# Wide-head attention written step by step, with queries and keys of two tiles at once in three split passes

## The chip, the cores and the metric

The kernel runs on one core of one Trainium2 chip. The metric is the device time of one execution in microseconds. TensorE is PE in the rows (PEld is its weight load), VectorE is DVE, ScalarE is ACT, GpSimd is POOL and SyncE is SP.

## What is computed

The reference is a stack of four layers, each a cross-attention or a mixture stage followed by a feed-forward stage, over 32 sequences of 64 rows with 128 features (2,048 rows). The stage that is changed is the attention of the second layer. Its shape, cut from the reference:

```python
DIM = 128
NUM_HEADS = 16
DIM_HEAD = 64
INNER = NUM_HEADS * DIM_HEAD
SCALE = DIM_HEAD ** (-0.5)
def _layernorm(x, gamma, beta, eps=1e-05):
    mu = jnp.mean(x, axis=-1, keepdims=True)
    var = jnp.mean(jnp.square(x - mu), axis=-1, keepdims=True)
    return (x - mu) * jax.lax.rsqrt(var + eps) * gamma + beta
```

A row is normalised twice (once outside, once with `gamma` and `beta`), projected to 1,024 query columns; the context of the same sequence is projected to 1,024 key and 1,024 value columns. Each of the 16 heads takes a softmax over the 64 keys of the sequence, and the 1,024 results are projected back to 128, scaled by a gate and added to the row.

## The kernel before

The 2,048 rows are 16 tiles of 128 rows (two sequences each). The stages run one after the other: A0 (attention with small heads), F0 (a feed-forward, during which a router for a later stage is worked out "beside" it), A1 (the wide-head attention that is changed, `wide_head_attention`), E1 (16 experts), then E2, E3, A3 and Q3. Every engine has one instruction queue, in program order, and the engines meet only through semaphores. What runs when is thus set by the order in which each engine's part of a stage is written.

A1 is a software pipeline. Every engine executes the same sequence of steps `n`, and in a step it serves several tiles at different stages of their way. In step n, PE does `scores(n-2)`, `turn_x(n-1)` (a transpose of the normalised tile), `turn_probs(n-3)`, `queries(n-1)`, `turn_out(n-4)`, `keys(n)`, `weigh_values(n-3)`, `project(n-4)` and `values(n-2)`. Queries and keys are 8 fp32 matmuls of 128x128 by 128 columns each, per tile. DVE does in step n: `x1` (the outer normalisation applied to tile n), the inner statistics, maximum and subtraction on the scores of tile n-2, the inner normalisation applied, the outer statistics of tile n+1, sum and reciprocal of the softmax, the scaling of the weighted values, the addition to X, and two copies of the values out of PSUM. POOL does `inner.rstd(n)`, `outer.rstd(n+1)` (a power on a 128x1 column, each waiting for DVE's statistics), and a copy of the context tile (`ctx1`) for `values`. ACT copies everything else out of PSUM and takes the exponentials. Steps 0 to 6 and 15 to 20 are written out; steps 7 to 14 are a loop of two steps per iteration (`pipeline`, L48), whose addresses and wait values come from registers. PSUM banks J0 and J1 are shared in turn by the turned x, queries, keys and values of a step; the waits in `keys`, `queries`, `turn_x` and `values` on `q_ready`, `k_ready` and `v_ready` hand them over.

In F0, products with 512 columns are already done in three passes of the type float32r (high times high, high times low, low times high): the low part of the input is made by POOL in `low_part` (L249), by a subtraction of two SBUF operands. POOL's part of F0 ends with the four `owners` (L1922) of the router, which take what DVE makes in `places` (L1910, L1914) and give it to PE's `table_products` (L1930). DVE's chain of small router operations (`choose`, L1818 to L1846), then the addition of the bias to X (L1687), then `slots` (L1876 to L1890) stand ahead of those in its queue; PE's `rank_products` (L1865) wait for the last link of `choose`.

## Time and profile before

| | us |
|---|---|
| median of 3 runs | 962.73 |
| lowest and highest | 961.08, 964.19 |
| span of the profiled execution, first to last instruction | 1010.8 |
| of it F0 (from the end of A0 at 100.0) | about 48 |
| of it A1, from its first product (148.36) to E1's first router product (344.08) | 195.7 |

Only the span is given for the profiled execution; it is 48 us longer than the median of the runs without a profile. In the span, PE is busy for 77%, DVE for 60%, ACT for 48% and POOL for 37%, and the chain that ended last is PE for 67%. These are averages over stages of very different kinds; A1 by itself is read from windows and the timeline. Times in the rows are microseconds from the span's start.

### The profile page before, as it was taken

What the parts mean: (1) busy time and instruction counts of PE and PEld (TensorE: products, weight loads), DVE (VectorE), ACT (ScalarE), POOL (GpSimd) and SP (SyncE); (2) the same over time, 40 slices, a digit from 0 to 9 for tenths busy, and PEclk for the clock granted to TensorE, in tenths of its full rate; (3) what the DMA queues carried; (4) which work ended last, traced back from release to release, by engine and by line L of the source; (5) the groups of instructions that cost most, each with busy time, mean ns of one, the idle gap of its engine ahead of it and who ended that gap; (6) DMA issues with size and microseconds to landing.
All of it is one profiled execution on the core that took longest, in us unless ns stands there. A gap on an engine that the chain in (4) does not pass through costs nothing.

```text
span 1010.8 us, 24129 instructions
## 1 busy us (share of the span) xinstructions
PE 783.2 (77%) x8041; PEld 646.4 (64%) x8041; DVE 608.2 (60%) x1568; ACT 486.4 (48%) x984; POOL 372.9 (37%) x492
## 2 busy tenths in 40 slices
PE   6998899999999789996477775667677559969005
PEld 3766787888888679985476664667676526644005
DVE  3886747777777667767353224632222368867895
ACT  3886434555444344432154435334444357745753
POOL 5663421111111331111566653155556535550810
PEclk9999699999999979999699989579989769978557
DMA  6300000000000000033332213101111300000001
GB/s 187 96 0 1 1 1 3 2 3 0 0 0 3 1 11 19 21 102 103 95 100 88 64 41 105 42 19 43 40 37 45 85 23 3 0 1 1 0 0 42
DMA packets 49218, 36.06 MB, mean 36 GB/s; under 512 B 7665, under 2 KB 44978, under 8 KB 49138
## 3 DMA queue, kind: packets, MB, share of 16 engines
q1 hardware_dynamic: 43420, 24.45, 8.5%
q0 software_dynamic: 4992, 10.23, 3.6%
q8 instruction: 48, 0.79, 0.3%
q10 hardware_dynamic: 726, 0.33, 0.1%
q14 instruction: 32, 0.26, 0.1%
HBM read 26.73 MB, written 8.26 MB: 35 GB/s over the span
## 4 chain that ended last, share of the span: by engine, by line
PE 67%; DVE 9%; another core or an unknown queue 6%; issue 5%; ACT 5%; DMA 3%; DVEq 2%; POOL 2%; ACTq 1%; SPq 1%; POOLq 0%
PE psum L2118 9%; PE psum L1464 7%; PE psum L2143 4%; PE psum L1034 3%; PE psum L976 3%; PE psum L954 3%; PE psum L939 3%; PE psum L2442 2%; PE psum L1431 2%; PE psum L1432 2%; PE psum L1433 2%; PE psum L323 2%; PE psum L1016 2%; PE psum L663 2%
## 5 line engine op out<-in xcount | busy, mean ns | idle before, releaser
L2118 PE MATMUL psum<-E_XT,E_weights 128*128 128x128 f32 x780 | 114.3, 298 | 52.4 <-ACT E_XT L2198 27.7
L2118 PEld LDWEIGHTS psum<-E_XT,E_weights 128*128 128x128 f32 x780 | 103.0, 209 | 61.2 <-ACT E_XT L2198 30.8
L2266 POOL DMA_INDIRECT y_scratch<-E_y,route_place_of x78 | 78.8, 1010 | 83.2 <-DVE E_y L2321 37.8
L2258 POOL DMA_INDIRECT E_rows<-rows_scratch,route_token_of x78 | 76.4, 979 | 32.1 <-issue 25.5
L1723 DVE SCALAR_TENSOR_TENSOR X<-psum,E_gates,X 128x128 f32<-128x128 f32 x256 | 71.7, 344 | 26.5 <-PE psum L1464 26.4
L1464 PEld LDWEIGHTS psum<-E_w,E_h 128*128 128x128 f32 x512 | 69.4, 198 | 11.5 <-issue 3.5
L2221 ACT ACTIVATE E_h<-psum,cols 128x128 f32<-128x128 f32 x156 | 44.5, 368 | 66.4 <-issue 31.3
L1548 ACT ACTIVATE E_h<-psum,cols 128x512 f32<-128x512 f32 x64 | 43.8, 687 | 67.8 <-PE psum L1433 67.7
L1464 PE MATMUL psum<-E_w,E_h 128*128 128x128 f32 x512 | 70.4, 282 | 4.8 <-DVE X L1723 3.8
L2311 DVE TENSOR_TENSOR E_h<-E_sg,psum 128x384 f32<-128x384 f32 x39 | 21.6, 554 | 77.5 <-remote 26.8
L203 POOL TENSOR_TENSOR rstd<-vareps,nhalf 128x4 f32<-128x4 f32 x24 | 24.6, 1029 | 75.0 <-DVE vareps L197 74.9
L235 PE MATMUL psum<-ident,xn 128*128 128x128 f32 x80 | 20.0, 400 | 35.9 <-ACT xn L226 24.5
L2143 PE MATMUL psum<-L1w,E_h 128*128 x312 | 44.4, 288 | 0.5 <-DVE E_y L2323 0.5
L150 POOL TENSOR_TENSOR A_A_inner_rstd<-A_A_inner_vareps,nhalf 128x1 f32<-128x1 f32 x16 | 8.7, 543 | 95.5 <-DVE A_A_inner_vareps L144 95.5
L788 POOL TENSOR_TENSOR A_kexp<-E_first,hmask 128x512 f32<-128x512 f32 x32 | 32.7, 1042 | 30.0 <-PE psum L663 29.9
L2431 PE MATMUL psum<-ident,Q_amax_rows 128*1 128x128 f32 x5 | 1.7, 332 | 52.1 <-DVE Q_amax_rows L2539 51.4
L235 PEld LDWEIGHTS psum<-ident,xn 128*128 128x128 f32 x80 | 14.0, 210 | 43.5 <-issue 21.5
L2323 DVE TENSOR_TENSOR E_y<-psum,E2b2all 128x128 f32<-128x128 f32 x39 | 11.3, 290 | 49.6 <-PE psum L2143 27.9
L2143 PEld LDWEIGHTS psum<-L1w,E_h 128*128 128x128 f32 x312 | 40.4, 202 | 1.0 <-issue 0.7
L2114 PE MATMUL psum<-ident,E_rows 128*128 128x128 f32 x78 | 22.8, 293 | 22.3 <-DMA E_rows<-rows_scratch,route_token_of 22.3
L2204 ACT ACTIVATE E_weights<-E_first 128x768 f32 x39 | 32.9, 843 | 14.2 <-issue 13.9
L1075 ACT ACTIVATE A_xnT<-psum,cols 128x128 f32<-128x128 f32 x16 | 7.3, 457 | 65.3 <-PE psum L964 65.3
(346 smaller groups left out, 2160.2 us busy)
## 6 DMA issues: line engine op xcount, KB each, us to landing
routed_back<-y_scratch SPq DMA_DIRECT2D x16, 256.0 KB, 4.9
E_first<-in_L_xattn_W SPq DMA_DIRECT2D x1, 2048.0 KB, 8.6
L1w<-in_L_xattn_W SPq DMA_DIRECT2D x8, 256.0 KB, 4.7
rows_scratch<-xn SPq DMA_DIRECT2D x8, 256.0 KB, 2.3
E_w<-in_L_ffn_routed_w SPq DMA_DIRECT2D x28, 64.0 KB, 1.9
E_raw<-in_L_ffn_w_down SPq DMA_DIRECT2D x8, 176.0 KB
E_rows<-rows_scratch,route_token_of POOLq DMA_INDIRECT x78
y_scratch<-E_y,route_place_of POOLq DMA_INDIRECT x78
```

Source lines behind the costliest of these rows:

```text
L235: tr = pe.transpose(self.bank[:, i * P:(i + 1) * P], self.m.xn[:, g * GT + i, :], self.m.ident[:, :])
L788: ke = pool.tensor_tensor(kexp[:, p, b], kk.broadcast_to([P, HP, S]), m.hmask[:, :].rearrange("p (h o) -> p h o", o=1).broadcast_to([P, HP ...
L939: mm = pe.matmul((J1, J0)[j][:, c * P:(c + 1) * P], w["k"][:, cc * P:(cc + 1) * P], columns(m.ctxT, t, P), start=True, stop=True)
L1464: mm = pe.matmul(y_bank(e, g)[:, i * P:(i + 1) * P], h[:, g % 2, c, i * P:(i + 1) * P], w2[:, p, c, :], start=(c == 0 and i == 0), stop=(c ...
L1548: act.activation(h[:, g % 2, c, :], ring[(C * g + c) % 4], spec["func"], bias=spec["b1"][:, bass.ds(e * C + c, 1)]).then_inc(h_ready.sem, 1)
L1723: st = dve.scalar_tensor_tensor(out=m.X[:, t, :], in0=y_bank(e, g)[:, i * P:(i + 1) * P], scalar=gates[:, t, bass.ds(e, 1)], in1=m.X[:, t, :],
L2118: mm = pe.matmul(out[:, c * P:(c + 1) * P], WE[:, p, (k0 + c) * P:(k0 + c + 1) * P], XT[:, p, :], start=True, stop=True)
L2143: mm = pe.matmul(Y[p][:, 0:P], h[:, p, c, :], W2[:, bass.ds(e, 1), c, :].rearrange("p o d -> p (o d)"), start=c == 0, stop=c == C - 1)
L2204: act.activation(WE[:, i % 2, :], W1[:, bass.ds(e, 1), :].rearrange("p o f -> p (o f)"), ACT.Copy).then_inc(w_ready.sem, 1)
L2221: ac = act.activation(h[:, p, c, :], m.banks[2 + i % 3][:, c * P:(c + 1) * P], spec["func"], bias=spec["b1"][:, bass.ds(e * C + c, 1)])
L2258: pool.indirect_dma_start(out=xg[:, i % 4, :], out_offset=None, in_=rows[:, :], in_offset=bass.IndirectOffsetOnAxis(ap=disp.token_of[:, i: ...
L2266: pool.indirect_dma_start(out=yrows[:, :], in_=y[:, i % 3, :], in_offset=None, out_offset=bass.IndirectOffsetOnAxis(ap=disp.place_of[:, i: ...
```

## The change

A1 is written out for all its steps, 23 instead of 21, without a loop. The weights of queries and keys are split into a high part (rounded to float32r, made by ACT in two copies of 128x1024 ahead of F0) and a low part (made by POOL in two subtractions of 128x1024, written between F0's `low_part` and its `owners`). The context is split by four ACT copies of 128x512 (`CH`) after F0's ACT work, and four POOL subtractions of 128x512 (`CL`) ahead of A1's first `outer.rstd`. The normalised tile is copied out of PSUM by two ACT activations instead of one (`xH`, `xnT`), and POOL subtracts them (`x_low`, 128x128), as the third thing of its step, where the copy of the context tile stood. Queries and keys are made for a pair of tiles at once: in each step half of a pair's keys and half of a pair's queries, 4 blocks of 3 passes by 256 columns each. So `scores` runs four steps behind `x1` instead of two. `queries` of a pair need the low parts of both its tiles: in an even step n, that of tile n-1, which the same step turns. The keys of the first pair stand ahead of A1's start. Large buffers are laid over others that are free at the time (F0's weights move to a place of their own for it), and `values` reads the context itself.

```diff
-def wide_head_attention(sh, m, tag, start, w):
...
+def wide_head_attention(sh, m, tag, start, w, split_weights):
...
-        qT = sb("qT", [P, 2, HP, P])
-        ctx1 = sb("ctx1", [P, 2, P])
-        kT = sb("kT", [P, 2, HP, 2, S])
+        q_odd = sb("qT", [P, HP, PW])
+        k_odd = sb("kT", [P, HP, PW])
...
+    qT = [m.xn[:, :, :].rearrange("p t d -> p (t d)").rearrange("p (c q) -> p c q", q=PW), q_odd]
+    kT = [m.XNT[:, :].rearrange("p (c k) -> p c k", k=PW), k_odd]
+    xH, xL = (m.split_rows[:, i, :].rearrange("p (r q) -> p r q", q=PW) for i in range(2))
+    CH, CL = m.split
+    WH, WL = m.wide_high, m.wide_low
...
     def tensor(pe):
-        m.begin(pe, start)
         pe.wait_ge(*m.dispatch.owner_ready(1))
-
-        def keys(t, p):
+        pe.wait_ge(*split_weights)
+
+        def three(out, wk, cc, xs, start=True):
+            ws = slice(cc * P, (cc + 1) * P)
+            pe.matmul(out, WH[:, wk, ws], xs[0], start=True, stop=False)
+            pe.matmul(out, WH[:, wk, ws], xs[1], start=False, stop=False)
+            return pe.matmul(out, WL[:, wk, ws], xs[0], start=False, stop=True)
+
+        def keys(i, n):
+            pair, half = i // 2, i % 2
+            cols = slice(pair * PW, (pair + 1) * PW)
+            pe.wait_ge(*ctx_low(pair // 2 + 1))
             for j in range(2):
-                if past(t, 1):
-                    pe.wait_ge(*q_ready(2 * t - 1 + j))
-                for c in range(4):
-                    cc = 4 * j + c
-                    mm = pe.matmul((J1, J0)[j][:, c * P:(c + 1) * P], w["k"][:, cc * P:(cc + 1) * P],
-                                   columns(m.ctxT, t, P), start=True, stop=True)
+                if i == 1:
+                    pe.wait_ge(*k_ready(j + 1))
+                elif i >= 2 and j == 1:
+                    pe.wait_ge(*xnT_ready(n))
+                elif i >= 2 and n >= 5:
+                    pe.wait_ge(*v_ready(2 * (n - 5) + 1))
+                elif i >= 2:
+                    pe.wait_ge(*q_ready(2 * (n - 3) + 1))
+                for c in range(2):
+                    mm = three((J1, J0)[j][:, c * PW:(c + 1) * PW], 1, 4 * half + 2 * j + c, (CH[:, cols], CL[:, cols]))
                 mm.then_inc(k_ps.sem, 1)
 
...
+        def turn_x(t, n, p):
+            pe.wait_ge(*xn_ready(t + 1))
+            if n >= 5:
+                pe.wait_ge(*v_ready(2 * (n - 5) + 2))
...
+            pe.transpose(J0[:, 0:P], xn[:, p, :], m.ident[:, :]).then_inc(xnT_ps.sem, 1)
+
+        def queries(i, n):
+            pair, half = i // 2, i % 2
+            r = pair % 2
+            pe.wait_ge(*x_low(2 * pair + 2))
...
+                for c in range(2):
+                    mm = three((J1, J0)[j][:, c * PW:(c + 1) * PW], 0, 4 * half + 2 * j + c, (xH[:, r, :], xL[:, r, :]))
+                mm.then_inc(q_ps.sem, 1)
...
                 for u in range(2):
-                    mm = pe.matmul((J1, J0)[b][u * S:(u + 1) * S, :], ctx1[:, p, b * S:(b + 1) * S], wv[:, :, u, :],
-                                   start=True, stop=True)
+                    mm = pe.matmul((J1, J0)[b][u * S:(u + 1) * S, :], m.ctxT[:, t * P + b * S:t * P + (b + 1) * S],
+                                   wv[:, :, u, :], start=True, stop=True)
                 mm.then_inc(v_ps.sem, 1)
...
+        for i in range(2):
+            keys(i, 0)
+        m.begin(pe, start)
+
...
-            if begun(n) and n == NT + 2:
+            if is_tile(n - 4):
+                scores(n - 4)
+            if is_tile(n - 1):
+                turn_x(n - 1, n, q)
+            if is_tile(n - 5):
+                turn_probs(n - 5, q)
...
+            if 3 <= n <= NT:
+                keys(n - 1, n)
+            if is_tile(n - 6):
+                turn_out(n - 6, p)
+            if is_tile(n - 2):
+                queries(n - 2, n)
+            if is_tile(n - 5):
+                weigh_values(n - 5, q)
+            if after(tag) and n == NT + 5:
+                after(tag).turn(pe, 1)
+            if is_tile(n - 6):
+                project(n - 6, p)
+            if is_tile(n - 4):
+                values(n - 4, n)
+
+        steps(step)
...
     def scalar(act):
+        for s, n in first_products_done:
+            act.wait_ge(s, n)
+        for g in range(NG):
+            cols = slice(g * GW, (g + 1) * GW)
+            act.activation(CH[:, cols], m.ctxT[:, cols], ACT.Copy).then_inc(ctx_high.sem, 1)
+
+        def keys_kept(i):
+            pair, half = i // 2, i % 2
+            if pair >= 2:
+                act.wait_ge(*scores_ready(2 * pair - 2))
+            for j in range(2):
+                c = 4 * half + 2 * j
+                act.wait_ge(*k_ps(2 * i + j + 1))
+                act.activation(kT[pair % 2][:, c:c + 2, :].rearrange("p c k -> p (c k)"), (J1, J0)[j],
+                               ACT.Copy).then_inc(k_ready.sem, 1)
+
+        for i in range(2):
+            keys_kept(i)
         m.begin(act, start)
...
+            if is_tile(n - 1):
                 t = n - 1
                 act.wait_ge(*xnT_ps(t + 1))
-                if past(t, 2):
-                    act.wait_ge(*q_ps(2 * t - 2))
+                if t >= 4:
+                    act.wait_ge(*q_ps(4 * (t // 2) - 4))
+                act.activation(xH[:, t // 2 % 2, t % 2 * P:(t % 2 + 1) * P], J0[:, 0:P], ACT.Identity, bias=w["beta"],
+                               scale=w["gamma"])
+                if t >= 2:
+                    act.wait_ge(*x_low(t - 1))
                 act.activation(xnT[:, q, :], J0[:, 0:P], ACT.Identity, bias=w["beta"],
                                scale=w["gamma"]).then_inc(xnT_ready.sem, 1)
...
-        pipeline(act, step, LO, HI, END)
+            if after(tag) and NT + 4 <= n < NT + 6:
+                after(tag).evacuate(act, n - NT - 4)
+
+        steps(step)
...
     def gpsimd(pool):
+        for g in range(NG):
+            cols = slice(g * GW, (g + 1) * GW)
+            pool.wait_ge(*ctx_high(g + 1))
+            pool.tensor_tensor(CL[:, cols], m.ctxT[:, cols], CH[:, cols], ALU.subtract).then_inc(ctx_low.sem, 1)
         m.begin(pool, start)
...
         def step(n, p):
-            if live(n):
+            if is_tile(n):
                 inner.rstd(pool, n, p, xn_ready)
-            if live(n + 1):
+            if is_tile(n + 1):
                 outer.rstd(pool, n + 1, 1 - p, x1_ready)
-            if live(n - 1):
-                context(n - 1, 1 - p)
+            if is_tile(n - 1):
+                t = n - 1
+                at = slice(t % 2 * P, (t % 2 + 1) * P)
+                pool.wait_ge(*xnT_ready(t + 1))
+                pool.tensor_tensor(xL[:, t // 2 % 2, at], xnT[:, 1 - p, :], xH[:, t // 2 % 2, at],
+                                   ALU.subtract).then_inc(x_low.sem, 1)
 
         outer.rstd(pool, 0, 0, x1_ready)
-        pipeline(pool, step, LO, HI, END)
-        if begun(NT):
+        steps(step)
...
-                t = n - 2
+            if is_tile(n - 4):
+                t = n - 4
                 dve.wait_ge(*scores_ready(t + 1))
...
                 split(pool, e + 1, 1)
         if beside:
+            spec["pool_between"](pool)
...
+        with ExitStack() as early:
+            m.wide_low = early.enter_context(nc.sbuf_tensor("L1w_low", [P, 2, 1024], F32R))
...
+        with ExitStack() as early:
+            m.split_rows = early.enter_context(nc.sbuf_tensor("A1_xnT_split", [P, 2, 4 * P], F32R))
+        with ExitStack() as early:
+            f0_weights = early.enter_context(nc.sbuf_tensor("F0_weights", [P, 2, 4 * P], F32))
+            m.wide_high = early.enter_context(nc.sbuf_tensor("L1w_high", [P, 2, 1024], F32R))
...
+        wide_high_ready, wide_low_ready = sem("wide_high_ready"), sem("wide_low_ready")
+
+        def low_parts(pool):
+            for i, k in enumerate((1, 0)):
+                pool.wait_ge(wide_high_ready, i + 1)
+                pool.tensor_tensor(m.wide_low[:, k, :], wide[:, k, :], m.wide_high[:, k, :], ALU.subtract
+                                   ).then_inc(wide_low_ready, 1)
+
...
+                            "F0": (f0_weights[:, 0:1, :], f0_weights[:, 1:2, :].rearrange("p o (c d) -> p o c d", d=D))}
...
+            for k in (1, 0):
+                act.activation(m.wide_high[:, k, :], wide[:, k, :], ACT.Copy).then_inc(wide_high_ready, 1)
```

POOL's queue at the end of F0 and the start of A1, before (`F_XL` is F0's low part, `route_A` the owners, the `rstd` rows the normalisation of A1's tiles, `A_ctx` the copied context tile):

```order
L249 TENSOR_TENSOR F_XL<-XNT,F_XH 128x512 x3
L1922 TENSOR_TENSOR route_A<-route_is_block,token_number 128x320 x4
L150 TENSOR_TENSOR A_A_outer_rstd<-A_A_outer_vareps,nhalf 128x1
L150 TENSOR_TENSOR A_A_inner_rstd<-A_A_inner_vareps,nhalf 128x1
...
L1124 COPY A_ctx<-ctxT 128x128
```

The same queue now (`L1w_low` is the low part of the weights, `E_XL` as written here the low part of the context, `A_xnT_split` the low part of a normalised tile):

```order
L249 TENSOR_TENSOR F_XL<-XNT,F_XH 128x512 x3
L2913 TENSOR_TENSOR L1w_low<-L1w,L1w_high 128x1024 x2
L1971 TENSOR_TENSOR route_A<-route_is_block,token_number 128x320 x4
L1167 TENSOR_TENSOR E_XL<-ctxT,E_XH 128x512 x4
L150 TENSOR_TENSOR A_A_outer_rstd<-A_A_outer_vareps,nhalf 128x1
L150 TENSOR_TENSOR A_A_inner_rstd<-A_A_inner_vareps,nhalf 128x1
...
L1179 TENSOR_TENSOR A_xnT_split<-A_xnT,A_xnT_split 128x128
```

Two subtractions came in ahead of the owners, four ahead of A1's first normalisation, and one per tile behind the two `rstd` of its step.

PE's queue in one full step of A1, before (`A_qT`, `A_kT` are queries and keys in SBUF, `A_on` the scaled result, `A_oT` the same turned):

```order
L990 MATMUL psum<-A_kT,A_qT 64x64 x32
L964 MATMUL psum<-ident,A_xn 128x128
L1001 MATMUL psum<-ident,A_prob 128x128 x8
L976 MATMUL psum<-A_xnT,L1w 128x128 x8
L1027 MATMUL psum<-ident,A_on 128x128 x8
L939 MATMUL psum<-ctxT,L1w 128x128 x8
L1016 MATMUL psum<-A_v,A_probT 64x64 x32
L1034 MATMUL psum<-L1w,A_oT 128x128 x8
L954 MATMUL psum<-L1w,A_ctx 64x512 x4
```

And in one full step now; of four blocks of keys (`E_XH`, `E_XL`) and four of queries (`A_xnT_split`) the first three passes stand (`XNT` and `xn` hold every second pair's keys and queries):

```order
L1013 MATMUL psum<-XNT,xn 64x64 x32
L971 MATMUL psum<-ident,A_xn 128x128
L1024 MATMUL psum<-ident,A_prob 128x128 x8
L940 MATMUL psum<-E_XH,L1w_high 128x256
L941 MATMUL psum<-E_XL,L1w_high 128x256
L942 MATMUL psum<-E_XH,L1w_low 128x256
...
L1050 MATMUL psum<-ident,A_on 128x128 x8
L940 MATMUL psum<-A_xnT_split,L1w_high 128x256
L941 MATMUL psum<-A_xnT_split,L1w_high 128x256
L942 MATMUL psum<-A_xnT_split,L1w_low 128x256
...
L1039 MATMUL psum<-A_v,A_probT 64x64 x32
L1057 MATMUL psum<-L1w,A_oT 128x128 x8
L998 MATMUL psum<-L1w,ctxT 64x512 x4
```

Keys and queries changed places around the turning of the result; the other rows stand as they stood.

## Rows read from the trace of the kernel before

**Rows 1.** Windows: stretch, length, busy time per engine, PEclk (granted clock), DMA share, GB/s.

```profile
173.40:314.50 141.10, 140.23 (x2418) 118.51 (x2416) 107.82 (x217) 69.40 (x120) 15.29 (x35) 1.00 0.01 1
```

**Rows 2.** Timeline of PE, a written-out step of A1: start, length, instruction, count.

```profile
185.97 1.16 PE L990 MATMUL psum<-A_kT,A_qT 64*64 64x64 f32 x64
...
188.10 1.95 PE L976 MATMUL psum<-A_xnT,L1w 128*128 128x128 f32 x16
...
189.89 1.04 PE L1027 MATMUL psum<-ident,A_on 128*128 128x128 f32 x8
...
190.76 1.95 PE L939 MATMUL psum<-ctxT,L1w 128*128 128x128 f32 x16
...
192.65 1.16 PE L1016 MATMUL psum<-A_v,A_probT 64*64 64x64 f32 x64
...
197.59 1.16 PE L990 MATMUL psum<-A_kT,A_qT 64*64 64x64 f32 x64
```

**Rows 3.** Timeline of E1: three passes by 512 columns, one after the other.

```profile
376.90 0.48 PE L1431 MATMUL psum<-E_XH,E_WH 128*128 128x512 f32 x1
377.21 0.40 PE L1432 MATMUL psum<-E_XL,E_WH 128*128 128x512 f32 x1
377.45 0.39 PE L1433 MATMUL psum<-E_XH,E_WL 128*128 128x512 f32 x1
```

**Rows 4.** Timeline of DVE and POOL in the step of rows 2.

```profile
187.80 1.23 DVE L1157 TENSOR_REDUCE A_mx<-psum 128x16 f32<-128x1024 f32 x1
...
191.34 0.54 POOL L150 TENSOR_TENSOR A_A_outer_rstd<-A_A_outer_vareps,nhalf 128x1 f32<-128x1 f32 x1 [2.84 <-DVE A_A_outer_vareps L144]
```

**Rows 5.** Timeline of E1's start: POOL's subtraction of 128x128.

```profile
345.96 0.46 POOL L1581 TENSOR_TENSOR E_WL<-E_w,E_WH 128x128 fp32r<-128x128 f32 x1
```

**Rows 6.** Timeline of F0: POOL's last subtraction, and DVE's router chain.

```profile
117.00 1.27 POOL L249 TENSOR_TENSOR F_XL<-XNT,F_XH 128x512 fp32r<-128x512 f32 x1 [1.08 <-ACT XNT L243]
117.08 1.34 DVE L1837 SCALAR_TENSOR_TENSOR route_at<-route_first,route_logits 128x128 f32<-128x128 f32 x1
...
119.10 0.29 DVE L1821 TENSOR_TENSOR route_work<-route_work,rev 128x128 f32<-128x128 f32 x1
...
121.26 2.28 DVE L1687 TENSOR_TENSOR X<-X,F0b 128x2048 f32<-128x2048 f32 x1
```

**Rows 7.** Timeline of F0, later: the slots, the second owner, the first table.

```profile
124.18 0.17 DVE L1876 TENSOR_SCALAR route_ntile<-psum 128x8 f32<-128x8 f32 x1 [0.64 <-PE psum L1867]
...
132.71 0.72 POOL L1922 TENSOR_TENSOR route_A<-route_is_block,token_number 128x320 fp32r<-128x320 f32 x1 [0.61 <-DVE route_is_block L1914]
...
133.84 1.94 PE L1930 MATMUL psum<-route_A,route_B 128*128 128x40 f32 x16
```

**Rows 8.** Timeline where A1 begins: ACT's last of F0, then POOL, ACT, DVE.

```profile
145.47 0.22 ACT L1851 ACTIVATE route_gate<-route_gate 128x16 f32<-128x16 f32 x1
...
149.33 0.55 POOL L150 TENSOR_TENSOR A_A_outer_rstd<-A_A_outer_vareps,nhalf 128x1 f32<-128x1 f32 x1 [9.73 <-DVE A_A_outer_vareps L144]
...
149.64 0.60 ACT L1107 ACTIVATE A_kT<-psum 128x512 f32<-128x512 f32 x1 [3.96 <-PE psum L939]
...
149.91 0.34 DVE L154 TENSOR_SCALAR A_x<-X,A_A_outer_meanvar,A_A_outer_rstd 128x128 f32<-128x128 f32 x1 [0.76 <-POOL A_A_outer_rstd L150]
...
153.50 0.34 DVE L154 TENSOR_SCALAR A_x<-X,A_A_outer_meanvar,A_A_outer_rstd 128x128 f32<-128x128 f32 x1 [0.65 <-POOL A_A_outer_rstd L150]
```

**Rows 9.** Windows with the granted clock, columns as in rows 1.

```profile
349.70:356.00 6.30, 5.06 (x17) 4.24 (x18) 1.88 (x4) 1.53 (x3) 3.87 (x5) 0.50 0.00 1
581.20:584.60 3.40, 3.40 (x18) 3.40 (x17) 0.78 (x2) 1.14 (x4) 2.34 (x3) 0.50 0.15 43
593.10:596.50 3.40, 3.38 (x28) 3.32 (x29) 0.92 (x3) 1.14 (x4) 2.49 (x4) 1.00 0.23 60
```

**Rows 10.** Timeline of PE: the idle time (in brackets) ahead of such windows.

```profile
349.76 1.09 PE L235 MATMUL psum<-ident,xn 128*128 128x128 f32 x4 [2.93 <-issue]
...
580.22 1.21 PE L2118 MATMUL psum<-E_XT,E_weights 128*128 128x128 f32 x8 [2.08 <-DVE E_XT L2296]
```

225 lines of the change are left out of this document (96 added, 129 removed).

## The prediction

> **What bounds the kernel now.** I read the windows first. A1's twelve full steps, from the scores of tile 2 to those of tile 14, take 141.1 us, and PE is busy for 140.2 of them at a granted clock of 1.00 (2.4 GHz), DVE for 107.8, ACT for 69.4, POOL for 15.3 [rows 1]. So in A1 the end is set by PE's own queue, and a matmul saved there is time saved as long as PE waits for nobody. The timeline of a written-out step shows the queue [rows 2]: scores, turned x and turned probabilities 2.13 us (185.97 to 188.10), queries 1.79, turned result 0.87, keys 1.89, then weighted values, projection and values 4.94; together 11.62. The loop's steps come to about 0.14 more (141.1 / 12 = 11.76). DVE and POOL are off the path, but their place in the step matters below: POOL's `outer.rstd` starts 5.37 us after the scores and had waited 2.84 us for DVE's outer statistics, which stand behind the maximum and the subtraction on this step's scores [rows 4].
>
> **PE's saving.** A pair costs, for queries and keys, 8 blocks of 3 passes by 256 columns each. No row has 256 columns. The nearest are passes by 512 at intervals of 0.31 (the first after fp32) and 0.24 us [rows 3]. The bounds are half of that, 0.12, if time goes with columns, and 0.24, if it does not. I take 0.12: 512 columns at 2.4 GHz are 0.213 us, so nearly all of the interval is columns. 12 passes are 1.45 us where 16 fp32 halves took 1.79 to 1.89. A step that waits for nothing is 2.13 + 1.45 + 0.87 + 1.45 + 4.94 = 10.84.
>
> The rows of 512 columns run at 0.24. The Trainium skill (TensorE: Matmul & The Clock Gate, Back-to-back issue gap) gives columns / 2.4 + 2.5 ns, 0.216 for 512; the row is longer. By it, 256 columns would be 0.109 and 12 passes 1.31, and the forecast some 2.3 us lower; the row decides.
>
> **The wait that is added.** In an even step PE's queries need the low part of the tile turned in the same step. POOL makes it, behind `outer.rstd` of the next tile but one in its queue. That ends 5.37 + 0.54 = 5.91 us after the scores [rows 4], the subtraction of 128x128 is 0.46 [rows 5], and two handovers bring it to 6.5. PE reaches its queries at 2.13 + 1.45 + 0.87 = 4.45. It then stands 2.05 us, with weighted values, projection, values and the next scores behind it: 6.5 + 1.45 + 4.94 = 12.9. This length no longer holds the price of the keys. DVE can't come earlier: its maximum waits for this step's scores, and ahead of it stand the copies of the values, which end with PE's last step. In odd steps the pair's low parts are there. A pair is 12.9 + 10.84 = 23.7, against 23.2 to 23.5 before: what the passes save, the wait gives back.
>
> From step 6 (the first full one) to step 17 (no keys, as step 16 before) there are eleven steps: 6, 8, 10, 12 and 14 wait; in 16 no `outer.rstd` is left. 5 x 12.9 + 6 x 10.84 = 129.5, where twelve took 141.0: -11.5. The queries of the last step save 0.35. ACT copies the turned x twice now, ahead of the probabilities that PE waits for. One copy is at most 0.60 [rows 8], and only the six steps without the other wait could feel it: 0 to 3.6 in all; I take 0, since ACT is busy for half of rows 1.
>
> **What it costs ahead of that: F0.** POOL's subtractions of 512 columns take 1.27 us, and a DVE operation on two SBUF operands that fell on one ran 1.34 instead of 0.29, until POOL was through [rows 6]. The two subtractions of 1,024 columns (2.54 each) now follow at once. The first holds DVE's next such operation from 118.42 to 120.96, the second holds L1821, at 119.10 so far, until 123.79: +4.69. DVE's bias addition then ends at 128.23, and the slots begin at 128.27 instead of 124.18: +4.1 [rows 6, 7]. The first table on PE stands 0.4 behind the second owner, which stands on the slots [rows 7]; it moves by 4.1 and F0's end with it, since PE is packed from there on. Bounds: 0, if all of it is hidden, and 5.1, the whole length of the two.
>
> That a subtraction of 2.54 us holds DVE to its end no row shows; rows 6 show it for 1.27. The Trainium skill (SBUF — State Buffer, SBUF: two separate sides) says that the loser waits for the whole instruction. If it were held for 1.27 alone, F0 would move by 1.6, and the forecast be 2.5 us lower; I go by the whole.
>
> **The context's low parts.** ACT's last work of F0 ends at 145.69 + 4.1 = 149.8; a copy of 512 columns is 0.60 [rows 8]; POOL then subtracts four times 1.27, from 150.45 to 155.55, ahead of A1's first `outer.rstd`. That was at 149.33 and comes at 155.6: 2.2 on top of the 4.1. Bounds 0 and 5.1.
>
> **Filling the pipeline.** DVE's first `x1` is then at 156.2. Without scores in between a tile takes 3.59 us [rows 8], so tile 2 is at 163.4, `outer.rstd` of tile 3 ends at 166.95, the low part of tile 1 follows, and the first queries start at 167.5. PE has had 2.9 us of keys and two transposes in 15 us. After 2.93 us of idling a stretch at 0.50 (1.2 GHz) followed [rows 9, 10], so I put these queries at half clock, 2.7 us instead of 1.45. With the copies (0.60 each) and the next keys and queries handing J0 and J1 to each other, scores of tile 0 are at 175.7 (174.2 at full clock). From them to the next `outer.rstd`'s end is 1.2 + 4.08 (187.80 to 191.88, rows 4), so step 4's queries start at 181.6, after PE idled for 3.1 us. Queries, copy and values bring step 5 to 185.0; it has no projection and is 8.0 long. Step 6: 193.0. For the clock after the 3.1 us I add 1.7, what 3.4 us at 0.50 lose [rows 9]: 194.7. From `x1` that is 38.5; before it was 149.91 to 173.43, 23.5: +15.0. Bounds: +11.8 without the clock, +18 if it stays low until step 6.
>
> **Sum.** +4.1 + 2.2 + 15.0 - 11.5 - 0.35 = +9.4 us at E1's start, and nothing behind it changes. The span of the profile is 1010.8 and the median 962.73; A1 ran at full clock in the profile, so I add the sum as it is: 962.7 + 9.4 = 972.1. About 0.3% (2.9 us) is what a measurement here can tell from no change.
>
> **Rivals.**
> 1. The passes pay and the low part is no wait. The mechanism is A1's wait on `x_low`: it decides at 4.45 us after the scores. If DVE and POOL reach `outer.rstd` 2 us sooner than rows 4 show, all eleven steps are 10.84 (119.2, 10.3 less) and step 4's idling goes (4.8 less): 957.0, faster. For it speaks PE's busy share in rows 1; against it the order on POOL and DVE. 0.10.
> 2. F0 and the context hide: the table has slack, or POOL's subtractions find DVE on single operands. 6.3 less: 965.8. 0.15, half of it within 0.3%.
> 3. The clock falls in the stalls of the even steps too. After an idle time of 2.08 us the stretch 581.2 to 584.6 was at 0.50, after another of that kind (593.1) the clock stayed at 1.00 [rows 9, 10]. Five falls at 1.7: 980.6. 0.15.
> 4. The change doesn't do what it says, a pass of 256 costs the 0.24 of 512: 12 are 2.82, an odd step 13.6, an even one 14.3, together 153.1: 995.7. Against it the arithmetic of columns above. 0.05.
>
> **How the numbers follow.** The forecast, 972.1, holds 0.55; it spreads by the bounds of the fill and of F0 from 965 to 977. The range, 963 to 982, takes in rivals 2 and 3; it leaves out rivals 1 and 4 and little more. Faster by over 0.3%: rival 1, 0.10. Within: half of rival 2 and the forecast's lower edge, 0.10. Slower: 0.80.
>
> **What will show it.** In the changed profile: PE's idle time in even steps, some 2 us ahead of the queries' first pass, released by POOL's `A_xnT_split`, and none in odd ones; starts of scores 12.9 and 10.8 us apart in turn; passes 0.12 apart; DVE's L1821 and the one before it stretched to some 2 us; the first table near 137.9; A1's first `outer.rstd` near 155.6; PEclk 0.50 around 167. It is wrong if the low part lands before PE asks for it, or if the F0 chain takes the two subtractions in its stride.

## The result, and the profile after

| | before | after |
|---|---|---|
| median of 4 runs, us | 963.15 | 978.74 |
| lowest and highest | 961.08, 964.19 | 978.47, 981.53 |
| ratio, with its 95% interval | | 1.017 (1.014 to 1.020) |

The changed kernel is 15.6 us slower. Its profiled execution took 978.51 us, with a span of 976.8. The span of before was 48 us above its median, and behind the end of E1 its trace is 51 us longer than that of the changed kernel (518.8 against 467.7); so the two traces are compared stage by stage and no further than the end of E1.

The steady part first, from scores of tile 2 to scores of tile 14, as in [rows 1]. Window of the changed kernel, columns as there:

```profile
194.01:334.57 140.56, 130.41 (x2306) 107.80 (x2304) 102.87 (x197) 70.15 (x128) 14.95 (x30) 1.00 0.01 2
```

The stretch is 140.6 us, 141.0 before [rows 1]. PE's work fell from 140.2 to 130.4, and its idle time rose from 0.9 to 10.2: the passes pay, and the wait takes it back. An even step in the timeline (PE and POOL of step 6):

```profile
194.01 1.16 PE L1013 MATMUL psum<-A_kT,A_qT 64*64 64x64 f32 x64
...
199.39 0.54 POOL L150 TENSOR_TENSOR A_A_outer_rstd<-A_A_outer_vareps,nhalf 128x1 f32<-128x1 f32 x1 [2.85 <-DVE A_A_outer_vareps L144]
199.89 0.45 POOL L1179 TENSOR_TENSOR A_xnT_split<-A_xnT,A_xnT_split 128x128 fp32r<-128x128 f32 x1
...
200.40 0.39 PE L940 MATMUL psum<-A_xnT_split,L1w_high 128*128 128x256 f32 x1 [1.81 <-POOL A_xnT_split L1179]
200.62 0.28 PE L941 MATMUL psum<-A_xnT_split,L1w_high 128*128 128x256 f32 x1
200.74 0.28 PE L942 MATMUL psum<-A_xnT_split,L1w_low 128*128 128x256 f32 x1
...
206.96 1.16 PE L1013 MATMUL psum<-A_kT,A_qT 64*64 64x64 f32 x64
```

POOL's `outer.rstd` waits 2.85 us for DVE's variance, as before ([rows 4], 2.84). The low part stands behind it, and PE stands for that: 1.81 us, released by `A_xnT_split`. The step is 12.95 long, the odd one behind it 10.86. The passes are 0.12 apart.

F0, DVE's router chain and POOL beside it, then PE (compare [rows 6, 7]):

```profile
118.06 4.85 POOL L2913 TENSOR_TENSOR L1w_low<-L1w,L1w_high 128x1024 fp32r<-128x1024 f32 x2
118.61 2.04 DVE L1868 TENSOR_TENSOR route_work<-route_at,route_best 128x128 f32<-128x128 f32 x1
120.68 2.37 DVE L1870 TENSOR_TENSOR route_work<-route_work,rev 128x128 f32<-128x128 f32 x1
...
124.91 2.28 DVE L1736 TENSOR_TENSOR X<-X,F0b 128x2048 f32<-128x2048 f32 x1
...
124.96 0.49 PE L1914 MATMUL psum<-route_both,earlier 128*128 128x128 f32 x2 [1.50 <-DVE route_ahead L1893]
...
133.52 1.64 POOL L1971 TENSOR_TENSOR route_A<-route_is_block,token_number 128x320 fp32r<-128x320 f32 x1 [10.61 <-DVE route_is_block L1963]
```

Two DVE operations of the kind that takes 0.29 us [rows 6] took 2.04 and 2.37 beside POOL's two subtractions. The bias addition, at 121.26 before, starts at 124.91; and PE now idles for 1.50 us ahead of the router's products.

The first and the third owner and DVE's last addition of F0, before, and then the last two of these after:

```profile
130.46 1.64 POOL L1922 TENSOR_TENSOR route_A<-route_is_block,token_number 128x320 fp32r<-128x320 f32 x1 [12.19 <-DVE route_is_block L1914]
...
136.63 1.64 POOL L1922 TENSOR_TENSOR route_A<-route_is_block,token_number 128x320 fp32r<-128x320 f32 x1 [3.20 <-DVE route_is_block L1914]
...
147.62 0.69 DVE L1719 TENSOR_TENSOR X<-X,psum 128x512 f32<-128x512 f32 x1 [4.67 <-PE psum L1464]
```

```profile
138.35 1.64 POOL L1971 TENSOR_TENSOR route_A<-route_is_block,token_number 128x320 fp32r<-128x320 f32 x1 [1.87 <-DVE route_is_block L1963]
...
149.45 0.69 DVE L1768 TENSOR_TENSOR X<-X,psum 128x512 f32<-128x512 f32 x1 [4.67 <-PE psum L1512]
```

The first owner is 3.1 us later, the third 1.7 and the last addition 1.8 (0.1 more each, counted from the mark that follows below): POOL waited 3.20 us ahead of the third owner before and waits 1.87 now, so part of the delay ends there.

The beginning of A1 on POOL and DVE, and then PE in the fill (compare [rows 8]):

```profile
148.12 5.00 POOL L1167 TENSOR_TENSOR E_XL<-ctxT,E_XH 128x512 fp32r<-128x512 f32 x4 [6.79 <-ACT E_XH L1097]
...
150.84 0.15 DVE L144 TENSOR_SCALAR A_A_outer_vareps<-A_A_outer_meanvar 128x1 f32<-128x1 f32 x1
...
153.07 0.55 POOL L150 TENSOR_TENSOR A_A_outer_rstd<-A_A_outer_vareps,nhalf 128x1 f32<-128x1 f32 x1
```

```profile
156.13 0.30 PE L971 MATMUL psum<-ident,A_xn 128*128 128x128 f32 x1 [3.22 <-DVE A_xn L154]
159.49 0.47 PE L971 MATMUL psum<-ident,A_xn 128*128 128x128 f32 x1 [3.06 <-DVE A_xn L154]
165.00 0.58 PE L940 MATMUL psum<-A_xnT_split,L1w_high 128*128 128x256 f32 x1 [5.04 <-POOL A_xnT_split L1179]
165.38 0.41 PE L941 MATMUL psum<-A_xnT_split,L1w_high 128*128 128x256 f32 x1
165.60 0.42 PE L942 MATMUL psum<-A_xnT_split,L1w_low 128*128 128x256 f32 x1
...
173.33 1.16 PE L1013 MATMUL psum<-XNT,xn 64*64 64x64 f32 x64 [0.78 <-ACT xn L1152]
...
179.28 0.58 PE L940 MATMUL psum<-A_xnT_split,L1w_high 128*128 128x256 f32 x1 [2.66 <-POOL A_xnT_split L1179]
...
182.14 3.52 PE L998 MATMUL psum<-L1w,ctxT 128*64 128x512 f32 x8
```

The variance was there at 150.99, `outer.rstd` came at 153.07 behind the four low parts of the context. The first queries run at half clock (a granted clock of 0.50; passes 0.21 apart), after 5.04 us of idling, and so do step 4's queries and values (3.52 us for eight products that otherwise take 1.94), after 2.66.

E1 is 2.5 us shorter in these two traces. Windows of the changed kernel from E1's first expert product on:

```profile
373.33:377.33 4.00, 3.06 (x8) 1.96 (x9) 3.56 (x6) 2.18 (x3) 4.00 (x5) 0.60 0.01 2
377.33:381.33 4.00, 4.00 (x31) 3.74 (x31) 3.00 (x9) 1.63 (x3) 4.00 (x7) 1.00 0.00 0
```

and the same two stretches of the kernel before:

```profile
353.75:357.75 4.00, 3.06 (x8) 1.95 (x8) 3.56 (x6) 2.18 (x3) 4.00 (x5) 0.50 0.01 2
357.75:361.75 4.00, 4.00 (x16) 3.71 (x17) 3.01 (x9) 1.02 (x2) 4.00 (x7) 0.50 0.00 0
```

The same work, after the same 2.93 us of idling; the clock is back in the second window of the changed kernel and not yet in that of before. From E1's first router product to PE's first work on what E1 leaves behind it is 147.94 us before and 145.42 after. The change is not shown to be the cause: the second of these windows in two of the kernels that follow, e1 and then e6, with 148.42 and 145.32 us for the same code:

```profile
358.66:362.66 4.00, 4.00 (x16) 3.71 (x17) 3.01 (x9) 1.02 (x2) 4.00 (x7) 0.50 0.00 0
```

```profile
356.20:360.20 4.00, 4.00 (x31) 3.74 (x31) 3.01 (x9) 1.63 (x3) 4.00 (x7) 1.00 0.00 0
```

**All stages in one table.** F0 begins up to 3.8 us sooner or later from execution to execution, so I count from a mark, POOL's third `rstd` of F0 (its line L203, at 104.51 before and 104.40 after). The columns follow each other: to A1's first `outer.rstd`; from there to scores of tile 0, and to scores of tile 2 (the fill); from scores of tile 2 to 14; from there to E1's first router product; E1. The last but one is the sum without the column of tile 0, the last the median of the runs. The kernels e1 to e9 are the experiments below. Each batch of runs has its own runs of the kernel before, with medians of 963.15 (for the changed kernel), 962.38 (e1 to e4), 961.42 (e5 to e7) and 962.84 (e8 and e9); every ratio is to those of its batch. One of the four runs of e4 took 1187.3 us at a granted clock of 0.631 and is left out of its median.

| kernel | to rstd | tile 0 | tile 2 | 12 steps | tail | E1 | sum | median |
|---|---|---|---|---|---|---|---|---|
| before | 44.82 | 7.55 | 24.10 | 141.03 | 29.62 | 147.94 | 387.51 | 963.15 |
| after | 48.67 | 20.26 | 40.94 | 140.56 | 29.09 | 145.42 | 404.68 | 978.74 |
| e1, low part first | 48.64 | 17.49 | 32.67 | 129.97 | 29.08 | 148.42 | 388.78 | 961.53 |
| e2, weights late | 46.72 | 21.71 | 40.86 | 142.10 | 29.08 | 145.93 | 404.69 | 977.97 |
| e3, context spread | 46.80 | 22.05 | 42.60 | 140.60 | 29.08 | 145.25 | 404.33 | 979.75 |
| e4, clock kept | 51.67 | 19.05 | 36.93 | 142.11 | 29.08 | 145.47 | 405.26 | 979.97 |
| e5, context early | 49.73 | 20.27 | 40.72 | 140.61 | 29.07 | 145.29 | 405.42 | 981.08 |
| e6, three moves | 43.74 | 18.40 | 33.57 | 129.98 | 29.07 | 145.32 | 381.68 | 957.22 |
| e7, and clock | 43.75 | 15.92 | 31.08 | 129.97 | 29.09 | 147.48 | 381.37 | 956.14 |
| e8, e6 without e1 | 44.72 | 20.26 | 41.00 | 140.58 | 29.08 | 145.73 | 401.11 | 976.43 |
| e9, queries sooner | 44.31 | 15.13 | 31.05 | 129.97 | 29.09 | 145.30 | 379.72 | 956.47 |

At E1's start the changed kernel has lost 3.85 + 16.84 - 0.47 - 0.53 = 19.7 us; E1 is 2.5 shorter, which leaves 17.2 in these two executions, where the medians have 15.6. E1 is the same code in all of the rows. It takes 147.5 to 148.4 us in the three executions in which the clock came back late (before, e1, e7) and 145.3 to 145.9 in the other eight. So 2.5 us of a difference between two single traces can come of E1 alone; where the rest of the way from 19.7 to 15.6 lies, these two traces don't show.

### The profile page after: what moved, and what is told of

It is laid out like the page before. It is cut to its first block, busy times and chain, and to the rows that moved or that the text cites. A ratio compares the mean times of both kernels' runs of the same rounds, so it can differ in the third digit from the quotient of the medians.

```text
span 976.8 us, 23579 instructions
## 1 busy us (share of the span) xinstructions
PE 766.5 (78%) x7913; PEld 625.0 (64%) x7913; DVE 613.5 (63%) x1568; ACT 495.3 (51%) x1006; POOL 384.3 (39%) x498
## 4 chain that ended last, share of the span: by engine, by line
PE 48%; issue 19%; POOL 13%; DVE 9%; ACT 5%; DMA 4%; SPq 1%; ACTq 1%; DVEq 0%; POOLq 0%
PE psum L1512 7%; POOL y_scratch L2315 4%; PE psum L2167 4%; POOL E_rows L2307 4%; PE psum L2192 3%; PE psum L2491 2%; PE psum L323 2%; PE psum L1481 2%; PE psum L1479 2%; PE psum L1480 2%; PE psum L1057 2%; PE psum L373 2%; PE psum L1862 1%; PE psum L663 1%; PE psum L349 1%
## 5 line engine op out<-in xcount | busy, mean ns | idle before, releaser
L2167 PE MATMUL psum<-E_XT,E_weights 128*128 128x128 f32 x780 | 103.9, 282 | 1.5 <-DVE E_XT L2345 0.8
L2167 PEld LDWEIGHTS psum<-E_XT,E_weights 128*128 128x128 f32 x780 | 96.7, 198 | 2.9 <-DVE E_XT L2345 1.5
L203 POOL TENSOR_TENSOR rstd<-vareps,nhalf 128x4 f32<-128x4 f32 x24 | 24.6, 1029 | 92.9 <-DVE vareps L197 92.8
L2163 PE MATMUL psum<-ident,E_rows 128*128 128x128 f32 x78 | 22.8, 292 | 24.2 <-DMA E_rows<-rows_scratch,route_token_of 24.1
L1627 POOL CAST E_WH<-E_w 128x128 fp32r<-128x128 f32 x16 | 4.6, 290 | 89.4 <-DMA E_w<-in_L_ffn_routed_w 69.7
L2192 PE MATMUL psum<-E_last,E_h 128*128 x234 | 34.5, 284 | 5.9 <-DVE E_h L2360 2.6
```

Source lines behind the costliest of these rows:

```text
L203: pool.tensor_tensor(m.rstd[:, ts], m.vareps[:, ts], m.nhalf[:, :].broadcast_to([P, GT]), ALU.pow).then_inc(self.rstd_ready.sem, 1)
L2167: mm = pe.matmul(out[:, c * P:(c + 1) * P], WE[:, p, (k0 + c) * P:(k0 + c + 1) * P], XT[:, p, :], start=True, stop=True)
L2192: mm = pe.matmul(Y[p][:, 0:P], h[:, p, c, :], W2[:, bass.ds(e, 1), c, :].rearrange("p o d -> p (o d)"), start=c == 0, stop=c == C - 1)
```

## The experiments

**The low part first (e1).** Theory: PE's wait in even steps is POOL's order alone. Rival: the two banks that go through ACT would hold PE there anyway.

```diff
         def step(n, p):
-            if is_tile(n):
-                inner.rstd(pool, n, p, xn_ready)
-            if is_tile(n + 1):
-                outer.rstd(pool, n + 1, 1 - p, x1_ready)
             if is_tile(n - 1):
                 t = n - 1
...
                 pool.tensor_tensor(xL[:, t // 2 % 2, at], xnT[:, 1 - p, :], xH[:, t // 2 % 2, at],
                                    ALU.subtract).then_inc(x_low.sem, 1)
+            if is_tile(n):
+                inner.rstd(pool, n, p, xn_ready)
+            if is_tile(n + 1):
+                outer.rstd(pool, n + 1, 1 - p, x1_ready)
```

> POOL makes the low part of the turned tile at the head of its step, ahead of inner.rstd and outer.rstd; nothing else is changed against the changed kernel (978.7 us). Theory A, that the even steps' 1.8 us and step 4's 2.7 us on PE are POOL's queue order alone: the low part then lands about 3.3 us after the scores where PE asks at 4.4, scores stand 10.9 us apart in every step of the steady part (twelve steps 130.5 instead of 140.6, that is -10 to -12), step 4 loses its 2.7 us of idling and perhaps its half clock (-2.7 to -5.6), and the first queries start 3.7 us sooner because tile 1's low part no longer stands behind the third outer.rstd (-2 to -3.7). Together 957 to 963 us. Theory B, that the handover of the two banks through ACT (keys copied, then queries into the same bank) would hold PE there anyway: the idle time stays at about 1.8 us, now released by ACT, and the time stays within 4 us of 978.7.

Measured: 961.53 us, 17.2 less than the changed kernel, and 1.0005 of the kernel before (0.9975 to 1.0036). The steady part as a window, and step 6 in the timeline:

```profile
185.94:315.91 129.97, 129.08 (x2305) 107.63 (x2303) 102.92 (x197) 70.16 (x128) 14.95 (x30) 1.00 0.01 3
```

```profile
185.94 1.16 PE L1013 MATMUL psum<-A_kT,A_qT 64*64 64x64 f32 x64
...
188.28 0.46 POOL L1175 TENSOR_TENSOR A_xnT_split<-A_xnT,A_xnT_split 128x128 fp32r<-128x128 f32 x1 [4.85 <-ACT A_xnT L1124]
...
190.28 0.36 PE L940 MATMUL psum<-A_xnT_split,L1w_high 128*128 128x256 f32 x1
...
191.32 0.54 POOL L150 TENSOR_TENSOR A_A_outer_rstd<-A_A_outer_vareps,nhalf 128x1 f32<-128x1 f32 x1 [2.09 <-DVE A_A_outer_vareps L144]
...
196.81 1.16 PE L1013 MATMUL psum<-A_kT,A_qT 64*64 64x64 f32 x64
```

The low part is done 2.8 us after the scores, PE takes it at 4.34 without idling, and every step is 10.87 long: 10.6 us less in twelve. The fill is 8.3 us shorter, since tile 1's low part no longer waits for the third `outer.rstd` and step 4 no longer idles. The rival falls, and the time is within theory A's 957 to 963. The low part's place in POOL's queue cost 18.9 us up to E1's start, of the 19.7 lost there.

**The weights' low parts late (e2).** Theory: they hold the router's chain in F0, and that moves A1. Rival: the table has slack.

```diff
         if beside:
-            spec["pool_between"](pool)
             for j in range(NCH):
                 beside.owners(pool, j)
+            spec["pool_between"](pool)
```

> POOL's two subtractions of 1,024 columns (low parts of the weights) stand behind the four owner operations of F0 instead of ahead of them. Theory A, that they stretched two DVE operations of the table (2.04 and 2.37 us where 0.29 is usual) and that this moved the table by 3.05 us, F0's last addition by 1.8 and A1's first outer.rstd by the rest: those two operations are back at 0.29, the owners are back within 0.3 of 130.5 and 132.7, the context's low parts start at 145.1, A1's first outer.rstd is at 150.0 instead of 153.07, and the time is 975.7 (974.5 to 976.9). Theory B, that the table had slack and the context's low parts set A1's start for another reason: the owners move back, the first outer.rstd does not, and the time stays at 978.7.

Measured: 977.97 (ratio to before 1.0145, 1.0107 to 1.0182), above theory A's 974.5 to 976.9 and, by the interval, not to be told from the changed kernel. The trace tells more: the two DVE operations are back at 0.29 us, the first owner is 25.95 us after the mark, as before (25.95; after 29.12), PE doesn't idle ahead of the router's products, and `outer.rstd` is 1.95 us sooner, not 3.05. The context's low parts still stand ahead of it, and they wait for ACT's copies behind the read-out of the table, which moved by 1.96. In this execution the clock fell once in an even step; windows of step 6, which was 14.43 long and idled 1.82 us ahead of its queries:

```profile
189.98:196.00 6.02, 4.58 (x95) 4.27 (x93) 5.58 (x13) 3.84 (x8) 1.17 (x3) 1.00 0.01 3
196.00:198.00 2.00, 1.62 (x9) 1.62 (x10) 0.67 (x2) 0.24 (x1) 0.32 (x1) 0.71 0.00 0
198.00:200.00 2.00, 2.00 (x46) 1.77 (x48) 0.00 (x0) 1.38 (x3) 0.00 (x0) 0.50 0.00 0
200.00:202.00 2.00, 2.00 (x46) 1.93 (x41) 1.21 (x1) 0.52 (x1) 0.00 (x0) 0.94 0.03 8
```

That is 1.5 us, once. So theory A holds for the table, and its size for A1's start was less.

**The context's low parts spread (e3).** Theory: four in a row keep the first `outer.rstd` waiting. Rival: something else sets the fill.

```diff
...
+        context_low(0)
         m.begin(pool, start)
...
                 inner.rstd(pool, n, p, xn_ready)
+            if 1 <= n < NG:
+                context_low(n)
```

> Only the first of the context's four low parts stands ahead of A1's first outer.rstd on POOL; the other three follow one by one behind inner.rstd of tiles 1 to 3. Theory A, that the four in a row (5.0 us) kept outer.rstd waiting behind a variance that DVE had ready at 150.99: outer.rstd starts at 151.0 instead of 153.07, each later subtraction delays the next outer.rstd by 0.1 to 0.2, and the time falls by 1.5 to 2.1, to about 977. Theory B, that the fill of the pipeline is set by something other than that chain of tiles: outer.rstd moves and scores of tile 0 stay at 173.3, the time at 978.7. A third way: POOL's subtractions hold DVE's operations in the fill, which then costs 1 us or more per subtraction: 979 to 981.

Measured: 979.75 (ratio 1.0174, 1.0140 to 1.0209). `outer.rstd` starts 1.87 us sooner, and scores of tile 0 are where they were, counted from the mark. The time alone (977.20 to 980.97 in four runs) fits theory B's 978.7 as well as the third way's 979 to 981; the trace shows the third way's mechanism. DVE and POOL in the fill:

```profile
152.62 0.34 DVE L154 TENSOR_SCALAR A_xn<-A_x,A_A_inner_meanvar,A_A_inner_rstd 128x128 f32<-128x128 f32 x1 [0.67 <-POOL A_A_inner_rstd L150]
...
156.11 1.26 POOL L1167 TENSOR_TENSOR E_XL<-ctxT,E_XH 128x512 fp32r<-128x512 f32 x1
156.18 1.27 DVE L154 TENSOR_SCALAR A_xn<-A_x,A_A_inner_meanvar,A_A_inner_rstd 128x128 f32<-128x128 f32 x1 [0.66 <-POOL A_A_inner_rstd L150]
```

DVE's `xn`, the operation that POOL had just released, takes 1.27 us instead of 0.34 beside each of the three subtractions, and the chain from one tile to the next grows by 0.9 three times.

**The clock kept up in the fill (e4).** Theory: the half clock of the first queries comes of the idling. Rival: it doesn't.

```diff
             if is_tile(n - 1):
                 turn_x(n - 1, n, q)
+            if n == 2:
+                for _ in range(38):
+                    pe.matmul(pO[:, 0, 0:PW], WH[:, 1, 0:P], CH[:, 0:PW], start=True, stop=True)
```

and 24 of the same ahead of `turn_x` in steps 1 and 2.

> PE runs passes of 256 columns on the context in the idle time of the fill (24 ahead of each of the first two turned tiles, 38 ahead of the first queries), into banks that are written over later; the result is not used. Theory A, that the half clock of the first queries came of the idling ahead of them: the queries' passes stand 0.12 apart instead of 0.21 and scores of tile 0 come 1.2 us sooner. For step 4, whose idle time of 2.7 us is left as it is, two ways: its queries and values stay at half clock, the gain is 1.2 in all (977.5); or they run at full clock too, since the fill no longer idles, and the gain is 4.2 (974.5). Theory B, that the granted clock there has nothing to do with the idling: 978.7, or more where the added passes delay a turned tile.

Measured: 979.97 (ratio 1.0164, 1.0121 to 1.0208), no gain in the time, where theory A had 977.5 or 974.5. In the trace the fill is 4.0 us shorter: scores of tile 0 come 1.2 sooner, and step 4 runs at full clock, though its idle time of 2.66 us is still there; the second way of theory A. Two other places took it back in that execution: a step 6 of 14.45 as in e2 (1.5), and F0 (3.0), which is next.

**F0's clock, read from e4, e5 and e1.** The wait of PE ahead of the router's products in F0, 1.50 us in the changed kernel, came out at 2.71 us in e4, and at 2.74 in e5 and e1. Windows of e5 behind it, and the same of e1:

```profile
126.00:129.00 3.00, 2.50 (x11) 2.50 (x12) 2.90 (x6) 0.00 (x0) 0.00 (x0) 0.50 0.00 0
129.00:132.00 3.00, 3.00 (x17) 3.00 (x16) 2.66 (x11) 0.00 (x0) 0.00 (x0) 0.50 0.00 0
```

```profile
126.00:129.00 3.00, 3.00 (x29) 3.00 (x29) 2.76 (x8) 0.00 (x0) 0.00 (x0) 1.00 0.00 0
129.00:132.00 3.00, 3.00 (x18) 2.59 (x17) 2.76 (x9) 1.48 (x3) 0.00 (x0) 1.00 0.00 0
```

The same idle time, at the same place: the clock fell in e4 and e5, at a cost of 3 us, and stayed in e1.

**The context early (e5).** Theory: made while F0's last products run, the low parts cost nothing. Rivals: the fill absorbs it, or F0's last additions on DVE are held.

```diff
-    def scalar(act):
+    def context_high(act):
         for s, n in first_products_done:
             act.wait_ge(s, n)
         for g in range(NG):
             cols = slice(g * GW, (g + 1) * GW)
             act.activation(CH[:, cols], m.ctxT[:, cols], ACT.Copy).then_inc(ctx_high.sem, 1)
+    m.context_high = context_high
...
         if beside:
+            m.context_high(act)
             beside.table(act, J1)
```

> ACT rounds the context (four copies) right behind F0's last activations instead of behind the read-out of the table, so that POOL's four subtractions for the context's low parts run from about 142 to 147 while F0's last products run on PE; nothing else is changed against the changed kernel (978.7 us). Theory A, that these four kept A1's first outer.rstd waiting for 2.1 us behind a variance that was there, and that DVE has nothing in that stretch that they hold: outer.rstd starts within 0.2 us of its variance (150.99 where the rest stands as in the changed kernel), the intervals of the outer.rstd behind it stay at 3.6 (which the three spread subtractions had made 4.5), scores of tile 0 come 2.0 us sooner, and the time falls to 976.7 (975.5 to 977.5). Theory B, that the fill absorbs it: outer.rstd moves, scores of tile 0 do not, 978.7. Theory C, that the subtractions now hold F0's last additions on DVE: 978.7 to 981.

Measured: 981.08 (976.59 to 981.49; ratio 1.0193, 1.0163 to 1.0224). `outer.rstd` no longer waits for the low parts; it waited 4.31 us for its variance, and the intervals behind it are 3.6. Scores of tile 0 stand 20.27 us behind it, 20.26 in the changed kernel, so the fill absorbed nothing (theory B). But F0 itself was 3 us longer by the clock, in the profiled execution at least. That is not theory C: DVE's second addition of a product in F0 stood at 140.38, 3.1 us later by the mark than in the changed kernel, and the first subtraction came only at 146.31. So the time, above theory A's 975.5 to 977.5, says nothing on the move itself; the next runs do.

**The moves together (e6, e8).** Theory: the pieces add up. Rival: what is won ahead of A1 is lost again in the fill. e6 is e1, e2 and e5 in one; e8 leaves e1's move out.

> The low part at the head of POOL's step, the weights' low parts behind the owners and the context's roundings ahead of the table's read-out, all three together; the products are those of the changed kernel. Theory A, that the three are separate pieces of the loss: counted from F0's start, the first outer.rstd is back where the kernel before has it (the loss of 3.85 us there is gone), the fill and the steady part are as with the low part first alone (32.7 us from outer.rstd to scores of tile 2, 10.87 a step), and the time is 961.5 - 3.85 = 957.7 (956 to 959.5), 0.5% below the kernel before. Theory B, that what is won ahead of A1 is lost again in the fill, whose chain of tiles or clock sets scores of tile 2: 961.5, no different from the kernel before.

> Two of the three moves alone: the weights' low parts behind the owners and the context's roundings ahead of the table's read-out; the low part of the turned tile stays behind outer.rstd as in the changed kernel. This prices what the change put ahead of A1, which each move alone left open (977.97 and 981.08, within the spread of the changed kernel's own 978.5 to 981.5). Theory A, that the loss ahead of A1 is 3.85 us and comes back whole: the first outer.rstd stands where the kernel before has it, PE does not idle in F0 ahead of the table's first products, even steps stay at 12.95, and the time is 978.7 - 3.85 = 974.9 (973.5 to 976.5). Theory B, that the two moves were worth nothing without the third: 978.7.

Measured: e6 957.22 (ratio 0.9960, 0.9944 to 0.9975), e8 976.43 (1.0131, 1.0094 to 1.0167). In both, A1's first `outer.rstd` is 4.9 and 3.95 us nearer to the mark than in the changed kernel, at or ahead of where the kernel before has it, and PE doesn't idle ahead of the router's products. e6 came within 0.5 us of the expected 957.7. e8 stayed at the upper edge of its range: 2.3 us of the 3.9 show in the time. Up to E1's start e8 lost 15.8 us against before instead of 19.7.

**The clock on top (e7), and the queries sooner (e9).** e7 adds the unused passes of e4 to e6, 24, 24 and 10 of them. e9 moves, in the fill alone, the second half of the first pair's queries from step 3 to step 2, on PE and on ACT, with the waits on the two banks that follow from it. On PE:

```diff
-            if is_tile(n - 2):
-                queries(n - 2, n)
+            for i in {2: (0, 1), 3: ()}.get(n, (n - 2,)):
+                if is_tile(i):
+                    queries(i, n)
```

> The same three moves, and PE runs unused passes of 256 columns in the idle time of the fill (24 ahead of each of the first two turned tiles, 10 ahead of the first queries). Theory A: the first queries run at full clock (passes 0.12 apart, not 0.21) and scores of tile 0 come 1.2 us sooner than without; 956.5 (955 to 958). Theory B, that a later stretch idles instead, or that the fill waits for the tiles' chain on DVE and POOL and not for PE: scores of tile 0 stay, 957.7.

> The three moves and the unused passes as in the kernel of 956.1 us, and in the fill PE makes the second half of the first pair's queries right behind the first half, in step 2, and not behind the third tile's turned x and keys in step 3. Theory A, that what is left of the fill's loss (31.1 us from the first outer.rstd to scores of tile 2, where the kernel before takes 24.1) is the depth of the pipeline, work that stands ahead of the first scores in PE's queue: scores of tile 0 come 1.7 us sooner, the rest follows at the same distances, 954.5 (953.3 to 955.7). Theory B, that the tiles' chain on DVE and POOL sets the following steps: scores of tile 0 come sooner, scores of tile 2 do not, 956.1.

Measured: e7 956.14 (ratio 0.9943, 0.9924 to 0.9963), e9 956.47 (0.9936, 0.9913 to 0.9960). e7's tile 0 comes 2.5 us sooner than e6's, and the median 1.1: theory A, with a rather smaller gain in the time. e9's tile 0 comes 0.8 sooner (1.7 was expected), and tile 2 not at all. PE of e9 in step 5:

```profile
171.17 0.30 PE L971 MATMUL psum<-ident,A_xn 128*128 128x128 f32 x1 [0.70 <-DVE A_v L1259]
```

PE has reached the turned tile and waits for DVE, whose copy of the values frees the bank; theory B. What is left of the fill (31.1 us against 24.1) is thus not a matter of PE's order there alone. Whether DVE's chain by itself sets it, or the two extra steps as such, these runs leave open.

## Why the prediction came out as it did

972.1 was forecast, with 963 to 982, and 978.7 measured: slower, and inside the range, but a loss of 15.6 where 9.4 was worked out. The mechanism was the right one: the passes pay, and the low part on POOL takes it back. A count in the sum was wrong, and that the range holds all the same is in part luck. By its own steps:

- **The step that failed is a count.** "From step 6 (the first full one) to step 17 (no keys, as step 16 before) there are eleven steps", and then "129.5, where twelve took 141.0: -11.5". The prediction paired step 17 with step 16 of the kernel before because both are the first without keys. But scores run four steps behind now, and two before: scores of tile 14 stand in step 18, and from tile 2 to tile 14 there are twelve steps in either kernel. With twelve, its own lengths give 5 x 12.9 + 7 x 10.84 = 140.4, and -0.6 instead of -11.5; measured: 140.56, -0.47. The sum at E1's start would have been 20.3, and 983.0 the forecast, just above the range. 19.7 was lost there.
- **The lengths of the steps were right.** 12.95 and 10.86 were measured where 12.9 and 10.84 stood; the low part ended 6.3 us after the scores and PE took it at 6.39 (6.5). The price of a pass, 0.118, is the lower of the two bounds, by columns. The Trainium skill (TensorE: Matmul & The Clock Gate, Back-to-back issue gap) gives columns / 2.4 + 2.5 ns for an isolated matmul, which would make it an estimated 0.109. The trace does not agree, 0.118, and the row of 512 columns was the better guide. ACT's second copy cost nothing that shows in the odd steps (10.86), as taken.
- **F0 and the context's low parts** were put at 6.3 and came to 3.85. Each of the two subtractions did hold a DVE operation to its end (2.04 and 2.37 us). The Trainium skill (SBUF — State Buffer, SBUF: two separate sides) says that the one that comes second waits for the whole instruction, and the trace agrees, 2.37 beside a subtraction of 2.45. The table moved by 3.2, not 4.1: the two subtractions took 4.85 us and not 5.08, and the held operation was over 0.14 behind them, at 123.05 and not at 123.79. 0.3 of the prediction's 4.69 is a slip of its own: it sets the end of the hold against the former start of L1821 (119.10), not against its former end (119.39). The context's part, put at 2.2, came as 1.9. What was missed is that the end of F0 follows the table only in part: DVE's last addition of F0, and with it the first variance of A1, moved by 1.9 (147.62 to 149.45, and the 0.1 between the marks): POOL had waited for DVE ahead of the third owner, and that wait took up 1.3.
- **The fill** was put at 15.0 and took 16.84. Its pieces were the right ones (the queries behind tile 1's low part, at half clock; step 4's idling, 2.66 against 3.1; half clock after it). The clock's share, which the prediction put at 3.2, is 4.0 by e4. Most of the 1.8 that was missing lies in step 4 (12.26 us from scores to scores, where 9.3 and 1.7 for the clock stood) and step 5 (8.41 for 8.0). The prediction had tile 1's low part behind the third `outer.rstd`, but didn't price that apart: e1 took 8.3 us off the fill, half of its loss, by POOL's order alone.
- **"Nothing behind it changes" at E1's start** is not contradicted: E1 is 2.5 us shorter in the trace of the changed kernel, but the table has both lengths for the same code. The traces lose 19.7 at E1's start, which on 962.7 would be 982.4, just above the range; the medians lose 15.6. The forecast was less good than the range makes it look: the count left out 11.0 us and the fill 1.8, F0 with the context had 2.5 too many, and some 4 us that the traces have at E1's start are not in the times, of which 2.5 can be E1's clock in one trace and the rest is open.
- **Rival 1**, no wait for the low part, was put at 957.0, with the reason that decides: whether the low part is there 4.45 us after the scores. In the kernel as changed it isn't. e1 made it so, and took 10.6 us off the steady part where the rival has 10.3. **Rival 2** had half a point: the end of F0 hid 1.2 of the 3.2 us that the table moved by. Its other half, that POOL's subtractions might find DVE on single operands and hold nothing, does not hold everywhere: in e3 they held a DVE operation with one tensor operand. **Rival 3**, the clock falling in even steps, was seen once in e2 and once in e4 and in no step of the changed kernel's own trace, at 1.5 us each. **Rival 4** is out by the 0.118 us of a pass.

## What to carry to other kernels

When a product is made cheaper by splitting its operands, the operation that makes the low part can come to stand on the path, and its place in its own engine's queue can decide whether the saving is kept: here one subtraction moved ahead of two small powers on POOL was worth 17 us, more than the 11 that the passes save. When two pipelines of different depth are compared, pair their steps by the tile and the operation, not by the step that looks alike. And a subtraction on POOL that is "beside" the path should stand where DVE has nothing that it can hold.
